# Graph attention layer on one core: another step order on TensorE, Gelu built from tanh, and LayerNorm 2's root on GpSimd

## The chip, the core and the metric

The kernel runs on one core of one Trainium2 chip. The metric is device time in microseconds (us). Five engines work side by side, each in the order of its own program, and wait for each other with semaphores: TensorE (PE, matmuls), VectorE (DVE), ScalarE (ACT), GpSimd (POOL) and SyncE (SP, here for DMAs). Matmuls write to PSUM, which ScalarE and VectorE read.

## What is computed

```
x = x + softmax(where(adj != 0, q k^T * SCALE, -inf)) v @ w_proj + b_proj     # 8 heads of 16, q k v = layer_norm(x, g1, be1) @ w_qkv
h2 = layer_norm(x, g2, be2)
out = x + gelu(h2 @ w1 + b1) @ w2 + b2                                        # gelu(approximate=True), the tanh form
# x is 4096 x 128 float32, adj 4096 x 4096 int32, w1 128 x 512
```

## The kernel before

A prologue normalises x, makes k and v for all 4096 rows and the first q (about 121 us). Then tiles `i` of 512 query rows follow (TILES = 8), and one more round without attention finishes the last tile. A tile has 64 steps `g` (STEPS): four pairs of heads times 16 steps, and each step handles two blocks of 128 keys (BLOCKS = 2).

In a step TensorE makes for each block the scores of a pair of heads, keys on partitions, by adding a mask (L1010, "masks", four matmuls that run together) and q times k (L1023, "scores"). ScalarE takes the exponential of each block (L639, 128x1024). Every second step in pairs 0, 1 and 3, and every fourth in pair 2, block 1 has no mask matmuls; GpSimd clamps and masks its exponentials instead (L496, L502, in `mask_probs`, and L490 in pair 0). The value matmuls (L918, "values", `weigh_values`) run three steps behind the scores (LAG = 3) and add up in `pv_ps`. Exponentials lie in eight slots of `probs`.

The exponentials subtract a row maximum found ahead of time: each step also has four "row units" (L853, `row`), q times k with query rows on partitions, over which VectorE takes a masked maximum (L677). They belong to a pair of heads 21 steps on (AHEAD), so those of the last steps belong to the next tile. GpSimd splits the maxima into two parts (`split_max`), and TensorE and ScalarE put them in the q stack ("shift").

Two rings of PSUM banks set the order. The score ring has two places (a pair of banks each), taken in turn by block 0, block 1 and, in some steps, a fill; the masks of a place wait until ScalarE has taken the place two before (`score_turn`). The row ring has three banks; a unit waits until VectorE has taken the one three places before. "Fills" are the rest of the work, placed by tables of step numbers. On the score ring (ACT_FILLS): shifts, the transposes of LayerNorm 2's output (h2t), the hidden units of the MLP (up, four of 128x512) and the next tile's q (q, four). On the row ring (DVE_FILLS): sums and their way back (normalisation of a pair), the projection (proj) and the second MLP layer (down, two). For tile i-1, attention's end, projection, LayerNorm 2 and MLP run in the first half of tile i: projection in step 7, LayerNorm 2's statistics on VectorE right behind it (`layer_norm_stats`), its root on ScalarE in step 9 (L650), its application on VectorE in step 10, up in steps 13, 15, 17 and 19, Gelu over all four in step 21 (L645), down in steps 23 and 25.

In its step TensorE's program reads: masks of both blocks, scores of both blocks, row units 0 and 1, values, ACT fill, row units 2 and 3, DVE fill.

ScalarE needs a table loaded for some functions: the exponential, the root and Gelu each bring an ACT_TABLE_LOAD when the one before was another.

## Time and profile before

| what | value |
|---|---|
| median of 3 runs | 1943.15 us (1942.3 to 1944.14) |
| profiled execution | 1946.16 us |
| its span, first to last instruction | 1944.4 us |
| mean granted TensorE clock | 0.959 of full speed |
| first exponential of attention | 121 us |

Busy time is the union of the instructions of an engine. A row of a group gives the count, the busy time, the mean length of one in ns, and behind the second bar the idle time of the engine before it with what ended it. In a timeline a row gives start, length, engine, line and operation, and merged repeats as x2, x8. A pair of exponentials reads as one row of 2.12 us.

### The profile page before, as it was taken

Reading aid. Unit: us, or ns where it says so; the run is one execution under the profiler, and the core shown is the slowest. Engines: PE = TensorE matmul, PEld = TensorE weight load, DVE = VectorE, ACT = ScalarE, POOL = GpSimd, SP = SyncE. Lnnn points to the kernel's source line nnn. Section 1 sums busy time; section 2 is a strip of 40 time slices with the busy share of each in tenths; the row PEclk is TensorE's granted clock in tenths of the full one; section 3 lists DMA queues with packets and bytes.
Section 4 is the critical chain, followed back from the end, with each engine's and each line's share of the span. In section 5 each row is a group of like instructions: output and inputs, shape, how many; then the busy total and the mean of one; then the engine's idle time right before and its main releaser. Section 6 shows DMA issues by size and latency. Waiting matters only on the chain.

```text
span 1944.4 us, 48355 instructions
## 1 busy us (share of the span) xinstructions
PE 1701.3 (87%) x18018; PEld 542.2 (28%) x18018; DVE 1456.3 (75%) x4495; ACT 1321.2 (68%) x1431; POOL 1128.1 (58%) x1058
## 2 busy tenths in 40 slices
PE   6988898889998889888998889888898889888876
PEld 3422222232232322322222322323223322223224
DVE  6888888768887588867887688876887678876601
ACT  4547777667767677676776677676776677766671
POOL 5945676437754476546764477545765477543340
PEclk9869999999999899999999999999999999999996
DMA  7700135002530034101440034200450024400000
GB/s 209 168 16 2 46 120 110 2 7 87 116 72 2 17 105 111 48 1 61 123 97 2 7 94 116 66 2 28 125 114 15 1 73 116 70 1 7 2 7 6
DMA packets 168705, 115.20 MB, mean 59 GB/s; under 512 B 139283, under 2 KB 149014, under 8 KB 168470
## 3 DMA queue, kind: packets, MB, share of 16 engines
q1 hardware_dynamic: 157718, 103.71, 21.8%
q10 hardware_dynamic: 10752, 8.39, 1.4%
q8 instruction: 143, 2.34, 0.5%
q14 instruction: 92, 0.75, 0.1%
HBM read 74.33 MB, written 4.19 MB: 40 GB/s over the span
## 4 chain that ended last, share of the span: by engine, by line
PE 44%; ACT 26%; issue 21%; DVE 8%; DMA 1%; ACTq 1%; SPq 0%; POOLq 0%; POOL 0%; DVEq 0%
ACT probs L639 21%; PE score_ps L1023 11%; PE score_ps L1010 8%; PE pv_ps L918 6%; PE ring_ps L853 5%; DVE masked_out L677 5%; PE ring_ps L974 2%; PE score_ps L941 2%; PE ring_ps L957 2%; PE ring_ps L951 2%; PE ring_ps L964 2%; PE score_ps L931 2%; ACT q_stack L535 1%; ACT hidden L604 1%; PE score_ps L877 1%
## 5 line engine op out<-in xcount | busy, mean ns | idle before, releaser
L677 DVE CUSTOM_DVE_ANT_0 masked_out<-ring_ps,row_mask 128x512 bf16<-128x512 f32 x2048 | 1328.2, 689 | 307.8 <-PE ring_ps L853 250.8
L639 ACT ACTIVATE probs<-score_ps,score_scale 128x1024 f32<-128x1024 f32 x1024 | 1084.6, 1110 | 501.6 <-PE score_ps L1023 488.3
L918 PE MATMUL pv_ps<-probs,v_ones 128*17 128x512 f32 x4096 | 552.0, 612 | 2.9 <-POOL probs L502 2.9
L496 POOL TENSOR_SCALAR probs<-probs 128x1024 f32<-128x1024 f32 x224 | 232.9, 1040 | 481.6 <-ACT probs L639 478.3
L502 POOL TENSOR_TENSOR probs<-probs,keep 128x1024 f32<-128x1024 f32 x224 | 478.2, 2135 | 40.7 <-POOL probs L496 28.9
L853 PE MATMUL ring_ps<-k_stack,q_stack 51*64 51x512 f16 x4096 | 455.6, 400 | 33.5 <-DVE row_max L677 33.1
L1010 PE MATMUL score_ps<-mask_t,ident_bf 64*64 64x512 bf16 x3200 | 331.9, 393 | 98.1 <-ACT probs L639 77.4
L1023 PE MATMUL score_ps<-q_stack,k_stack 51*64 51x512 f16 x4096 | 346.3, 396 | 66.1 <-ACT probs L639 37.8
L853 PEld LDWEIGHTS ring_ps<-k_stack,q_stack 51*64 51x64 f16 x4096 | 149.0, 106 | 481.9 <-DVE row_max L677 400.0
L1023 PEld LDWEIGHTS score_ps<-q_stack,k_stack 51*64 51x64 f16 x4096 | 103.6, 105 | 265.5 <-ACT probs L639 98.9
L677 DVE DVE_READ_ACCUMULATOR2_ANT row_max<- 128x1 f32 x2048 | 170.3, 83 | 0.0
L1010 PEld LDWEIGHTS score_ps<-mask_t,ident_bf 64*64 64x64 bf16 x3200 | 91.2, 105 | 246.6 <-ACT probs L639 191.1
L437 POOL TENSOR_SCALAR row_mask<-row_mask 128x1024 bf16<-128x1024 bf16 x124 | 129.6, 1045 | 23.9 <-POOL row_mask L433 23.9
L433 POOL TENSOR_SCALAR row_mask<-adj_in 128x1024 bf16<-128x1024 uint32 x124 | 128.9, 1040 | 12.3 <-DVE row_max L677 5.3
L918 PEld LDWEIGHTS pv_ps<-probs,v_ones 128*17 128x17 f32 x4096 | 68.4, 96 | 192.7 <-issue 186.1
L518 POOL TENSOR_TENSOR q_stack<-q_x,q_neg 128x512 f16<-128x512 f32 x28 | 32.5, 1160 | 63.1 <-ACT q_x L597 63.1
L442 POOL TENSOR_SCALAR max_unit<-neg_max 128x4 f32<-128x4 f32 x64 | 12.7, 198 | 95.0 <-DVE neg_max L687 90.1
L774 DVE RECIPROCAL recip<-ring_ps 128x8 f32<-128x8 f32 x32 | 6.5, 203 | 64.0 <-PE ring_ps L951 64.0
L535 ACT COPY q_stack<-score_ps 2x256 f16<-2x256 f16 x128 | 46.5, 363 | 9.5 <-PE score_ps L820 7.2
L974 PE MATMUL ring_ps<-w_sb,hidden 128*128 128x128 f32 x256 | 46.1, 335 | 2.8 <-DVE row_max L677 1.5
L788 DVE TENSOR_TENSOR rows<-ring_ps,x_res 128x256 f32<-128x256 f32 x16 | 6.8, 425 | 55.0 <-PE ring_ps L976 55.0
L490 POOL TENSOR_SCALAR keep<-mask_t 128x512 bf16<-128x512 bf16 x64 | 39.5, 617 | 5.5 <-ACT probs L639 0.2
(92 smaller groups left out, 894.5 us busy)
## 6 DMA issues: line engine op xcount, KB each, us to landing
adj_in<-adj SPq DMA_DIRECT2D x128, 512.0 KB, 4.1
xnT_dram<-attn ACTq DMA_DIRECT2D x8, 256.0 KB, 3.6
mask_t<-row_mask SPq DMA_TRANSPOSE x128, 3.4
xq<-xnT_dram ACTq DMA_DIRECT2D x8, 256.0 KB, 2.7
x_res<-x ACTq DMA_DIRECT2D x8, 256.0 KB, 3.6
out<-rows ACTq DMA_DIRECT2D x8, 256.0 KB, 2.3
w_sb<-L_gnn_w SPq DMA_DIRECT2D x2, 256.0 KB
probs<-x SPq DMA_DIRECT2D x1, 256.0 KB, 2.9
```

The lines of the kernel that those rows point to most:

```text
L433: nc.gpsimd.tensor_scalar(target, adj_in[:, half, :].bitcast(U32), 1.0, 0.0, ALU.min, ALU.max)\
L437: nc.gpsimd.tensor_scalar(target, target, BIG, -BIG, ALU.mult, ALU.add).then_inc(mask_done, 1)
L496: nc.gpsimd.tensor_scalar(flat, flat, 128.0, 0.0, ALU.min, ALU.max).then_inc(probs_bounded, 1)
L502: nc.gpsimd.tensor_tensor(view, view, keep[:, m // 4, :].unsqueeze(1).broadcast_to([128, 2, TILE]), ALU.mult).then_inc(probs_masked, 1)
L535: last = nc.scalar.copy(stack[r:r + SHIFT_PARTS, p, 256 * jj:256 * (jj + 1)], bank.bitcast(F16)[r:r + SHIFT_PARTS, 0:256])
L639: nc.scalar.activation(probs[:, (2 * g + n) % SLOTS, :], score_ps[:, half:half + 2, :].rearrange("p a n -> p (a n)"), ACT.Exp, scale=score ...
L677: nc.vector.tensor_tensor_reduce(out=masked_out[:, place % 3, :], in0=ring_ps[:, place % 3, :], in1=row_mask[:, j, ch * 512:(ch + 1) * 512 ...
L853: last = nc.tensor.matmul(ring_ps[64 * t:64 * (t + 1), place % 3, :], stack[rows, p, first:first + 64], k_stack[rows, p, ch, K_FIRST:], st ...
L918: last = nc.tensor.matmul(pv_ps[32 * k:32 * k + HD + 1, :], v_ones[:, BLOCKS * (g % QUARTER) + b, 2 * p + a, :], probs[:, (2 * g + b) % SL ...
L974: nc.tensor.matmul(bank[:, 128 * s:128 * (s + 1)], hidden[:, f, 128 * t:128 * (t + 1)], w2_sb[:, f, :], start=(f == 0), stop=False)
L1010: last = nc.tensor.matmul(bank[to, :], ident_bf[keys, keys], mask_t[keys, source, :], start=True, stop=False)
L1023: last = nc.tensor.matmul(bank[64 * t:64 * (t + 1), :], k_stack[rows, p, m // 4, at + 64 * t:at + 64 * (t + 1)], q_stack[par][rows, p, :], ...
```

## The change

- In a step TensorE issues block 0's masks, row units 0 and 1, block 0's scores, block 1's masks and scores, row units 2 and 3, then values and both fills.
- Gelu is no longer one function of ScalarE over 128x2048. Per hidden unit f, ScalarE writes z = h + b (`hidden`) and z squared (`bent`), GpSimd makes z (0.7979 + 0.0357 z^2) (`bend`, two operations of 128x512), ScalarE takes tanh of it two steps later, GpSimd makes z (0.5 tanh + 0.5) (`gate`, two operations). In the last round, without attention, ScalarE's Gelu stays.
- LayerNorm 2's 1/sqrt: VectorE makes a first guess from the bits of var + eps (two operations), GpSimd runs three Newton steps of four operations on 128x4 (`root2`). VectorE applies it two subtiles in step 10, two in step 11.
- Fills move: up to steps 15, 17, 19, 21; h2t to 12 and 13; down to 27 and 29; q to 28, 31, 34 and 40. The load of x for the residual moves from step 0 to 2, the aggregates of LayerNorm 2 to the head of step 8, the store to 30.

TensorE, an even and an odd step of a middle tile without fills. L1010 or L1091 are masks, L1023 or L1104 scores, L853 or L934 row units, L918 or L999 values, each row with four matmuls per block or pair of units. Before:

```order
L1010 MATMUL score_ps<-mask_t,ident_bf 64x512 x8
L1023 MATMUL score_ps<-q_stack,k_stack 64x512 x8
L853 MATMUL ring_ps<-k_stack,q_stack 64x512 x4
L918 MATMUL pv_ps<-probs,v_ones 17x512 x4
L853 MATMUL ring_ps<-k_stack,q_stack 64x512 x4
L1010 MATMUL score_ps<-mask_t,ident_bf 64x512 x4
L1023 MATMUL score_ps<-q_stack,k_stack 64x512 x8
L853 MATMUL ring_ps<-k_stack,q_stack 64x512 x4
L918 MATMUL pv_ps<-probs,v_ones 17x512 x4
```

And of the change:

```order
L1091 MATMUL score_ps<-mask_t,ident_bf 64x512 x4
L934 MATMUL ring_ps<-k_stack,q_stack 64x512 x4
L1104 MATMUL score_ps<-q_stack,k_stack 64x512 x4
L1091 MATMUL score_ps<-mask_t,ident_bf 64x512 x4
L1104 MATMUL score_ps<-q_stack,k_stack 64x512 x4
L934 MATMUL ring_ps<-k_stack,q_stack 64x512 x4
L999 MATMUL pv_ps<-probs,v_ones 17x512 x4
L1091 MATMUL score_ps<-mask_t,ident_bf 64x512 x4
L934 MATMUL ring_ps<-k_stack,q_stack 64x512 x4
L1104 MATMUL score_ps<-q_stack,k_stack 64x512 x8
L934 MATMUL ring_ps<-k_stack,q_stack 64x512 x4
L999 MATMUL pv_ps<-probs,v_ones 17x512 x4
```

The values no longer stand between the two pairs of row units, and block 1's masks stand behind block 0's scores.

GpSimd of the change, steps 18 to 20 of a middle tile (before, only the probs and max rows are there). `bent` and `hidden` rows at L523 and L526 are a bend, at L534 and L537 a gate; the probs rows are one masked block, the max rows a split:

```order
L523 TENSOR_SCALAR bent<-bent 128x512
L526 TENSOR_TENSOR bent<-bent,hidden 128x512
L534 TENSOR_SCALAR bent<-bent 128x512
L537 TENSOR_TENSOR hidden<-bent,hidden 128x512
L508 TENSOR_SCALAR probs<-probs 128x1024
L514 TENSOR_TENSOR probs<-probs,keep 128x1024
L454 TENSOR_SCALAR max_unit<-neg_max 128x4
L458 CAST max_part<-max_unit 128x4
L461 TENSOR_TENSOR max_part<-max_unit,max_part 128x4
L523 TENSOR_SCALAR bent<-bent 128x512
```

A bend and a gate now stand in front of the masked block of their step. ScalarE of the change around the same place, where before one Gelu stood between two table loads:

```order
L707 ACTIVATE probs<-score_ps,score_scale 128x1024 x2
L668 ACTIVATE hidden<-score_ps,b_col 128x512
L669 ACTIVATE bent<-score_ps,b_col 128x512
L715 ACTIVATE bent<-bent 128x512
L707 ACTIVATE probs<-score_ps,score_scale 128x1024 x2
```

No table load stands in the order of the change between the first exponential and the last round.

The step tables:

```diff
-ACT_FILLS = {11: ("h2t", 0), 12: ("h2t", 1), 24: ("q", 0), 27: ("q", 1), 33: ("q", 2), 40: ("q", 3)}
-ACT_FILLS.update({13 + 2 * f: ("up", f) for f in range(FC)})
+UP_STEPS = [15 + 2 * f for f in range(FC)]
+ACT_FILLS = {12: ("h2t", 0), 13: ("h2t", 1), 28: ("q", 0), 31: ("q", 1), 34: ("q", 2), 40: ("q", 3)}
```

GpSimd, the root and the calls in its step loop:

```diff
+            def root2(i):
+                first = (i - 1) * ROOT_OPS
+                pool.wait_ge(ln2_step, (i - 1) * LN2_STEPS + LN2_STATS)
...
+                for k in range(NEWTON):
...
+                    nc.gpsimd.tensor_tensor(newton[:, :], rstd[:, :], rstd[:, :], ALU.mult).then_inc(root_step, 1)
+                    pool.wait_ge(root_step, first + 4 * k + 1)
...
+                    if d and g == AGGR_STEP:
+                        root2(i)
+                    if d and c and g - 1 in UP_STEPS:
+                        bend(i, bcd, UP_STEPS.index(g - 1))
+                    if d and c and g - 3 in UP_STEPS:
+                        gate(i, UP_STEPS.index(g - 3))
```

ScalarE:

```diff
+                elif what[0] == "up" and bcd[1]:
+                    f = what[1]
+                    n = (i - 1) * FC + f
+                    if n >= 2:
+                        act.wait_ge(gelu_done, n - 1)
+                    nc.scalar.activation(hidden[:, f, :], bank, ACT.Identity, bias=b1_col[:, f:f + 1])
+                    nc.scalar.activation(bent[:, f % 2, :], bank, ACT.Square, bias=b1_col[:, f:f + 1])\
+                      .then_inc(score_taken, 1)
...
-                    if d and c and g == GELU_STEP:
-                        nc.scalar.activation(hidden[:, :, :].rearrange("p f n -> p (f n)"),
-                                             hidden[:, :, :].rearrange("p f n -> p (f n)"),
-                                             ACT.Gelu_apprx_tanh).then_inc(gelu_done, 1)
-                    if d and g == SQRT_STEP:
-                        act.wait_ge(ln2_step, (i - 1) * LN_STEPS + LN_STATS)
-                        nc.scalar.activation(rstd[:, :], inv_var[:, :], ACT.Sqrt).then_inc(rstd_done, 1)
+                    if d and c and g - 2 in UP_STEPS:
+                        f = UP_STEPS.index(g - 2)
+                        act.wait_ge(bent_done, 2 * ((i - 1) * FC + f) + 2)
+                        nc.scalar.activation(bent[:, f % 2, :], bent[:, f % 2, :], ACT.Tanh).then_inc(tanh_done, 1)
```

TensorE's step:

```diff
                 for g in range(STEPS):
                     if c:
-                        for n in range(BLOCKS):
-                            masks(g, n)
-                        for n in range(BLOCKS):
-                            scores(g, n)
+                        masks(g, 0)
                     for x in range(UNITS // 2):
+                        row(g, x)
+                    if c:
+                        scores(g, 0)
+                        masks(g, 1)
+                        scores(g, 1)
+                    for x in range(UNITS // 2, UNITS):
                         row(g, x)
...
                         weigh_values(i, bcd, g - LAG)
                     if g in act_fills:
                         act_fill(i, bcd, g, act_fills[g])
-                    for x in range(UNITS // 2, UNITS):
-                        row(g, x)
                     if g in dve_fills:
                         dve_fill(i, bcd, g, dve_fills[g])
```

## Rows read from the trace of the kernel before

**Rows 1.** The page, busy time of the engines.

```profile
PE 1701.3 (87%) x18018; PEld 542.2 (28%) x18018; DVE 1456.3 (75%) x4495; ACT 1321.2 (68%) x1431; POOL 1128.1 (58%) x1058
```

**Rows 2.** The page's groups, ScalarE's exponentials: busy, mean ns, idle before.

```profile
L639 ACT ACTIVATE probs<-score_ps,score_scale 128x1024 f32<-128x1024 f32 x1024 | 1084.6, 1110 | 501.6 <-PE score_ps L1023 488.3
```

**Rows 3.** Timeline, two plain steps: start, length, instruction, idle before.

```profile
954.45 0.39 PE L853 MATMUL ring_ps<-k_stack,q_stack 51*64 51x512 f16 x4
954.47 2.12 ACT L639 ACTIVATE probs<-score_ps,score_scale 128x1024 f32<-128x1024 f32 x2 [0.80 <-PE score_ps L1023]
...
954.77 1.05 PE L918 MATMUL pv_ps<-probs,v_ones 128*17 128x512 f32 x8
955.02 0.69 DVE L677 CUSTOM_DVE_ANT_0 masked_out<-ring_ps,row_mask 128x512 bf16<-128x512 f32 x1 [0.29 <-issue]
...
955.75 0.43 PE L853 MATMUL ring_ps<-k_stack,q_stack 51*64 51x512 f16 x4
...
955.99 0.40 PE L1010 MATMUL score_ps<-mask_t,ident_bf 64*64 64x512 bf16 x4
...
956.64 0.63 PE L1023 MATMUL score_ps<-q_stack,k_stack 51*64 51x512 f16 x8 [0.25 <-ACT probs L639]
...
957.16 2.12 ACT L639 ACTIVATE probs<-score_ps,score_scale 128x1024 f32<-128x1024 f32 x2 [0.58 <-PE score_ps L1023]
...
960.08 2.12 ACT L639 ACTIVATE probs<-score_ps,score_scale 128x1024 f32<-128x1024 f32 x2 [0.80 <-PE score_ps L1023]
```

**Rows 4.** Line L645, Gelu: lengths, first and last start.

```profile
L645 ACT ACTIVATE hidden<-hidden x7: 1910/1912/1914, 407.0 to 1758.3; 128x2048 f32<-128x2048 f32 x7
```

**Rows 5.** Timeline of TensorE, the fills.

```profile
792.56 1.05 PE L951 MATMUL ring_ps<-sum_sel,attn 128*128 128x2 f32 x8
...
803.11 3.84 PE L964 MATMUL ring_ps<-wp_pad,attn 128*128 128x128 f32 x32 [0.21 <-DVE row_max L677]
...
836.23 1.12 PE L941 MATMUL score_ps<-h2T,w_sb 128*128 128x512 f32 x2
...
868.52 1.16 PE L974 MATMUL ring_ps<-w_sb,hidden 128*128 128x128 f32 x8
...
870.02 1.16 PE L974 MATMUL ring_ps<-w_sb,hidden 128*128 128x128 f32 x8
```

**Rows 6.** Timeline, LayerNorm 2's statistics on VectorE.

```profile
806.99 0.69 DVE L781 TENSOR_TENSOR x_res<-ring_ps,x_res 128x512 f32<-128x512 f32 x1 [2.62 <-PE ring_ps L964]
...
809.51 0.69 DVE L677 CUSTOM_DVE_ANT_0 masked_out<-ring_ps,row_mask 128x512 bf16<-128x512 f32 x1
```

**Rows 7.** Timeline, GpSimd's masking, the root's table load, units; behind Gelu.

```profile
815.10 2.12 POOL L502 TENSOR_TENSOR probs<-probs,keep 128x1024 f32<-128x1024 f32 x1 [0.17 <-issue]
815.23 1.28 ACT L639 ACT_TABLE_LOAD   x1
...
818.73 0.40 PE L853 MATMUL ring_ps<-k_stack,q_stack 51*64 51x512 f16 x2 [2.56 <-DVE row_max L677]
...
866.12 1.91 PE L918 MATMUL pv_ps<-probs,v_ones 128*17 128x512 f32 x8
```

**Rows 8.** Line L331, LayerNorm's application: ns min/median/max.

```profile
L331 DVE TENSOR_SCALAR rows<-x_res,mean_var,rstd x32: 333/335/2059, 362.5 to 1915.2; 128x128 f32<-128x128 f32 x32
```

**Rows 9.** The page's groups, GpSimd.

```profile
L496 POOL TENSOR_SCALAR probs<-probs 128x1024 f32<-128x1024 f32 x224 | 232.9, 1040 | 481.6 <-ACT probs L639 478.3
L502 POOL TENSOR_TENSOR probs<-probs,keep 128x1024 f32<-128x1024 f32 x224 | 478.2, 2135 | 40.7 <-POOL probs L496 28.9
...
L518 POOL TENSOR_TENSOR q_stack<-q_x,q_neg 128x512 f16<-128x512 f32 x28 | 32.5, 1160 | 63.1 <-ACT q_x L597 63.1
```

**Rows 10.** Timeline, a small operation of GpSimd.

```profile
821.39 0.19 POOL L446 CAST max_part<-max_unit 128x4 f16<-128x4 f32 x1 [0.17 <-POOL max_unit L442]
```

**Rows 11.** Busy us (x count) by window, with granted clock (PEclk).

```profile
954.00:960.00 6.00, 5.47 (x72) 1.36 (x68) 5.64 (x19) 4.23 (x4) 3.62 (x4) 1.00 0.62 200
862.00:870.00 8.00, 5.52 (x38) 1.98 (x38) 3.63 (x11) 4.94 (x5) 2.07 (x2) 0.79 0.00 0
```

More of the change, by code:

```diff
@@ L602, in take_fill @@
                                          scale=gb[:, 2:3], bias=gb[:, 3:4]).then_inc(score_taken, 1)
+                elif what[0] == "up" and bcd[1]:
+                    f = what[1]
+                    n = (i - 1) * FC + f
+                    if n >= 2:
[3 more added lines that the diff above has]
+                      .then_inc(score_taken, 1)
                 elif what[0] == "up":
-                    nc.scalar.activation(hidden[:, what[1], :], bank, ACT.Identity if bcd[1] else ACT.Gelu_apprx_tanh,
+                    nc.scalar.activation(hidden[:, what[1], :], bank, ACT.Gelu_apprx_tanh,
                                          bias=b1_col[:, what[1]:what[1] + 1]).then_inc(score_taken, 1)
@@ L784, in take_fill @@
                     dve.wait_ge(row_taken, full)
-                    layer_norm_stats(lambda k: dve.wait_ge(ln2_step, (i - 1) * LN_STEPS + k), ln2_step, x_res)
+                    for s in range(SUB):
+                        nc.vector.bn_stats(stats[:, s, :], x_res[:, s, :]).then_inc(ln2_step, 1)
                 elif what[0] == "down":
@@ L795, in body @@
                 for g in range(STEPS):
[L796 to L798 removed]
+                    if d and g == AGGR_STEP:
+                        before = (i - 1) * LN2_STEPS
+                        dve.wait_ge(ln2_step, before + SUB)
+                        for s in range(SUB):
+                            nc.vector.bn_aggr(mean_var[:, s, :], stats[:, s, :]).then_inc(ln2_step, 1)
+                        dve.wait_ge(ln2_step, before + 2 * SUB)
+                        nc.vector.tensor_scalar(inv_var[:, :], mean_var[:, :, 1], EPS, None, ALU.add).then_inc(ln2_step, 1)
+                        dve.wait_ge(ln2_step, before + 2 * SUB + 1)
+                        nc.vector.tensor_scalar(half_bits[:, :], inv_var[:, :].bitcast(I32), 1, None,
+                                                ALU.logical_shift_right).then_inc(ln2_step, 1)
+                        dve.wait_ge(ln2_step, before + 2 * SUB + 2)
+                        nc.vector.tensor_scalar(rstd[:, :].bitcast(I32), half_bits[:, :], -1.0, ROOT_GUESS,
+                                                ALU.mult, ALU.add).then_inc(ln2_step, 1)
+                    if d and g in (APPLY_STEP, APPLY_STEP + 1):
+                        dve.wait_ge(root_step, i * ROOT_OPS)
+                        for s in range(2 * (g - APPLY_STEP), 2 * (g - APPLY_STEP + 1)):
+                            nc.vector.tensor_scalar(rows2[:, s, :], x_res[:, s, :], mean_var[:, s, 0:1], rstd[:, s:s + 1],
+                                                    ALU.subtract, ALU.mult).then_inc(ln2_step, 1)
                     if g < row_steps(b, c):
```

64 lines of the change are left out of this document (51 added, 13 removed).

## The prediction

> **What bounds the kernel now.** I read the page first. No engine is full: TensorE 87% busy by the modelled ends of its matmuls, VectorE 75%, ScalarE 68% [rows 1]. ScalarE's dearest group, the 1024 exponentials, waited 501.6 us, nearly all of it for the score matmuls [rows 2]. So an in-order handshake sets the time, and the timeline of a stretch without extra work has to be read.
>
> There [rows 3] a step is two exponentials (the pair 2.12 us), four row units and eight value matmuls. Exponential pairs start at 954.47, 957.16 and 960.08: steps of 2.69 and 2.92, mean 2.80. The cycle: both exponentials end, then the scores start on TensorE (956.64, released by ACT), then 0.52 us to the next exponential (957.16). TensorE issues both blocks' masks ahead of both scores, so block 0's scores wait for block 1's exponential of the step before: ScalarE idles 0.58 or 0.80 us in each step.
>
> Gelu's rows lie 225.2 us apart (407.0 to 1758.3, six intervals) [rows 4]: a middle tile. Its 64 steps at 2.80 make 179.2; the other 46.0 us are the work between steps (LayerNorm, MLP, next q, normalisation) and the waits it causes: VectorE's normalisation [rows 6], and ScalarE's tables and Gelu [rows 4, 7].
>
> **The new order, plain steps.** Now TensorE does: masks 0, row units 0 and 1, scores 0, masks 1, scores 1, units 2 and 3, values. The old wait is gone: scores 0 need only exponential 0 of the step before. What is late next? Unit 3 needs the bank of unit 0 (ring of three), and the values stand behind it. From the same rows: units start to first maximum 0.57 (954.45 to 955.02); the maximum 0.69; its end to the next units about 0.06 (955.71 to 955.75, the second half a little later); units to values 0.32 (954.45 to 954.77); values to next work 0.98 (to 955.75); masks to units 0.24 (taken from units to masks, 955.75 to 955.99). Sum 2.86 us for either kind of step. Before, the values lay between the two pairs of units and hid this round trip; now only scores and masks do (0.72 to 0.96 us of the 1.32). ScalarE fits: exponential 0 starts 0.76 after the units, exponential 1 ends at 2.88, the masks that need it come at 2.86 + 0.48. VectorE has 0.3 us left per step. So the reorder by itself gains nothing: 64 x 2.86 = 183.0, which is 3.8 worse.
>
> **Between the steps.** TensorE's work is unchanged, but now lies wholly on its path. From starts and durations [rows 5], less 0.07 for the overlap of modelled ends, as the values' 1.05 stand for 0.98 [rows 3]: a 512-column float32 fill 1.05 (1.12 less 0.07), eight of these (hidden, q) 8.4; sums 0.98 and their way back, taken the same and 0.07 on top, 8.2 for four (0.98 + 1.05 each); projection 3.8; second MLP layer 1.5 for each half of a fill (868.52 to 870.02), two fills, 6.0; transposes of h 0.7 and of shifts 1.7 (estimates: both are smaller than a fill, and a shift's next mask waits 0.2 for exponential 1). Together 28.8.
>
> Waits per tile:
> - LayerNorm 2's statistics on VectorE. From the addition to the first maximum 2.52 us (806.99 to 809.51) [rows 6]. Three small operations now follow the aggregates instead of two: + 0.2. Measured from the projection's end the maximum starts 2.8 later instead of 0.8: + 2.0.
> - The root. Removed: table, root, table on ScalarE. Added: 12 dependent 128x4 operations on GpSimd. A small one there takes 0.19 behind a wait of 0.17 for its forerunner [rows 10], 0.36, so 4.4 us with a hand-over. VectorE needs it two steps on, 5.4 us after the guess: covered. But GpSimd's masking of step 7 is queued behind it, 1.04 + 2.14 [rows 9], its half-size mask operation (about 0.6) and gaps = 4.2 more, and the values of step 7 wait for it in step 10: done 8.7 to 9.0 after the guess, wanted at 6.8. Take + 2.2 (bounds 0 and 4).
> - Normalising now in two halves, 0.6 each instead of one block, but see the lock below: inside that 2.2.
> - Hidden units: Identity and Square on ScalarE (0.6 to 0.7 each, estimated from Gelu's 1.91 for four times the columns plus a start-up) hold the score bank 1.4 instead of 0.8 us; the next masks 1 wait, and units 3 come 0.35 late, three times: + 1.0. The q fills hold it 1.3: + 0.5.
> - GpSimd's bend and gate. A 128x512 tensor_scalar lies between half of the 1024 form's 1.04 and all of it, and I take 0.6; for the tensor_tensor I take 1.16, the nearest row, between 1.07 (half of the 1024 form) and its whole 2.14 [rows 9]. With gaps a bend or gate is 2.1, so a pair of steps holds 4.2 + 3.4 for its masking = 7.6 us, against 7.1 (two steps and one fill and its wait). Four such rounds and a split (1.1) eat most of the 3.8 us of slack that a masked block has: + 1.5 (bounds 0 and 8).
> - TensorE's clock: it waited 2.56 us before 818.73, and behind Gelu the granted clock of the stretch was 0.79 [rows 11], eight value matmuls taking 1.91 instead of 1.05 (866.12) [rows 7]; that is the 1.2 GHz level for part of the stretch. The Gelu wait goes; the 2.5 us wait after the projection stays or grows. + 1.5 (bounds 0 and 3).
> Sum 8.7. Gone altogether are Gelu's 1.91 [rows 4] and four table loads of 1.28 (815.23 is one) [rows 7], 7.0 of ScalarE in a tile, and TensorE's stalls behind them.
>
> A tile: 183.0 + 28.8 + 8.7 = 220.5 against 225.2, so -4.7; six of them -28. The first tile has neither LayerNorm 2 nor MLP: it gains around its fills what it does not lose by 0.06 a step, -3 (estimate). In the last attention tile 20 steps have no row units; there nothing holds the values back, and ScalarE's 2.12 plus a short hand-over gives 2.2 instead of 2.80: -12, with -4 for the rest. The tail, on its own path, trades one root operation for 4.4 us: +4. Sum -43. The profiled execution took 1946.16 us (span 1944.4), 3 over the median; 1943.15 - 43 = 1900.
>
> **Two rules weighed.** A normalising tensor_scalar on VectorE has a median of 0.335 us and a maximum of 2.06 [rows 8]; GpSimd's tensor_tensor ran from 815.10 to 817.22 and TensorE waited until 818.73 for the row maxima queued behind the normalisation [rows 7]. The Trainium skill (SBUF — State Buffer, Who interferes with whom) says that such a VectorE operation and a GpSimd one exclude each other for the whole instruction; this trace agrees with 2.06 against 0.335. More GpSimd work means more such meetings: the two halves could each meet one.
> A table load takes 1.28 us in the row at 815.23 [rows 7]. The Trainium skill (ScalarE: Activation LUTs, What ACT_TABLE_LOAD costs) counts 2.66 for a switch with its drain. By that the tile would gain 5.5 us more (four times 1.38); I go by the row.
>
> **Rivals.**
> - GpSimd becomes the bound (slower). Place: steps 16 to 26, where a weigh waits for masked exponentials queued behind bends and gates, with ScalarE waiting for gates too. For it: 7.6 against 7.1 already; against: 58% busy over all, and the first two rounds start idle. If a float32 tensor_tensor costs 2.14, a round is 9.6 and four rounds lag 10, of which slack takes the first two: +8 a tile over my sum, seven tiles, 1956. It decides once bend and gate average above 2.9 us each.
> - The lock catches both halves: the first waits up to 2.1, beyond the 2.2 already counted 1.7, the second as much: 3.4 x 7 = 24, 1924.
> - TensorE's clock falls in ordinary steps, since it now pauses 0.4 to 0.6 us in each. A slow step costs about 1.5 more (values 1.91); every eighth step slow is 12 a tile: 1985. Against: the present plain stretch pauses as long per step, at clock 1.00 [rows 11].
> - The round trip is not on the path, since units 2 are issued early and the modelled ends hide overlap; then VectorE bounds, four maxima at 0.69 less 0.03 to 0.07 of overlap each, about 2.65: 0.2 x 450 steps, 1810. Against it: the ring of three banks leaves unit 3 no other bank, and the second pair starts 0.04 after the first maximum's end [rows 3].
>
> **Chances.** Forecast 0.66 (its bounds alone: 1878 to 1925), lock on both halves 0.12, faster still 0.06: together faster 0.84. GpSimd as the bound 0.08 and the clock 0.04: slower 0.12. Same 0.04, for a part of the GpSimd case that just eats the gain; a measurement of this kernel tells 0.2% (3.9 us) from no change. The range takes in the lock case and the near side of the GpSimd and faster cases: 1866 to 1938.
>
> **What would show it.** Plain steps of 2.86 us without alternation, exponentials starting before the earlier pair is done, "TensorE's row units wait for row_max" as the largest wait of TensorE; no Gelu or root tables in the middle; a wait of values for GpSimd's probs in steps 10 and 24. Plain steps of 2.65 or above 3.0 would make the forecast wrong, as would values waiting for GpSimd more than 5 us a tile.

## The result, and the profile after

The changed kernel takes 1914.43 us (median of 4 runs, 1913.38 to 1916.23), the kernel before 1943.64 on the same chips (4 runs, 1942.3 to 1946.99): a ratio of 0.9846, 95% interval 0.9834 to 0.9859. Forecast were 1900 us and a range of 1866 to 1938. The time is in the range, 14 us above the forecast. The profiled execution of the changed kernel took 1913.38 us, its span 1911.6, 32.8 shorter than the span before.

The page of the changed kernel, busy time of the engines and the largest groups with their waits (it answers to [rows 1], [rows 2] and [rows 9]):

```profile
PE 1737.2 (91%) x18018; PEld 547.8 (29%) x18018; DVE 1431.6 (75%) x4503; ACT 1298.9 (68%) x1443; POOL 1252.4 (66%) x1266
...
L707 ACT ACTIVATE probs<-score_ps,score_scale 128x1024 f32<-128x1024 f32 x1024 | 1087.8, 1112 | 457.3 <-PE score_ps L1104 454.8
...
L999 PE MATMUL pv_ps<-probs,v_ones 128*17 128x512 f32 x4096 | 542.6, 602 | 11.4 <-POOL probs L514 11.4
...
L934 PEld LDWEIGHTS ring_ps<-k_stack,q_stack 51*64 51x64 f16 x4096 | 168.3, 106 | 287.7 <-DVE row_max L742 242.1
...
L1104 PEld LDWEIGHTS score_ps<-q_stack,k_stack 51*64 51x64 f16 x4096 | 102.7, 104 | 341.6 <-PE score_ps L1091 325.3
```

Only 44 us of the exponentials' wait are gone (501.6 to 457.3). TensorE's busy share rose from 87 to 91% in a shorter span. GpSimd is 124 us busier and still not the bound.

The changed kernel's timeline, one plain step from exponential to exponential (it answers to [rows 3]; start, length, instruction, and in brackets the idle time before it with its releaser):

```profile
939.33 0.38 PE L934 MATMUL ring_ps<-k_stack,q_stack 51*64 51x512 f16 x2
...
939.39 2.12 ACT L707 ACTIVATE probs<-score_ps,score_scale 128x1024 f32<-128x1024 f32 x2 [0.76 <-PE score_ps L1104]
...
939.95 0.40 PE L934 MATMUL ring_ps<-k_stack,q_stack 51*64 51x512 f16 x2 [0.24 <-DVE row_max L742]
...
940.28 1.05 PE L999 MATMUL pv_ps<-probs,v_ones 128*17 128x512 f32 x8
...
941.27 0.41 PE L1091 MATMUL score_ps<-mask_t,ident_bf 64*64 64x512 bf16 x4
...
941.51 0.39 PE L934 MATMUL ring_ps<-k_stack,q_stack 51*64 51x512 f16 x4
...
941.75 0.11 PEld L1104 LDWEIGHTS score_ps<-q_stack,k_stack 51*64 51x64 f16 x4 [0.34 <-PE score_ps L1091]
...
942.07 0.69 DVE L742 CUSTOM_DVE_ANT_0 masked_out<-ring_ps,row_mask 128x512 bf16<-128x512 f32 x1 [0.34 <-issue]
942.27 1.11 ACT L707 ACTIVATE probs<-score_ps,score_scale 128x1024 f32<-128x1024 f32 x1 [0.76 <-PE score_ps L1104]
```

The step is 2.88 us (939.39 to 942.27), in even and odd steps alike (2.88 or 2.89). Unit 3 waits for the maximum (0.24), then 0.33 to the values, 0.99 to the next masks, 0.24 to the units: the path that the prediction summed. The row it had no term for is the weight load of the scores, which waits for the masks' end: masks start at 941.27, their scores at 941.75.

The changed kernel's timeline, TensorE's waits in steps 8 to 10 of the same tile as [rows 7]:

```profile
794.76 0.40 PE L934 MATMUL ring_ps<-k_stack,q_stack 51*64 51x512 f16 x2 [1.67 <-DVE row_max L742]
...
801.33 0.40 PE L934 MATMUL ring_ps<-k_stack,q_stack 51*64 51x512 f16 x2 [0.55 <-DVE row_max L742]
...
802.95 1.05 PE L999 MATMUL pv_ps<-probs,v_ones 128*17 128x512 f32 x8 [1.22 <-POOL probs L514]
```

Where the 32.8 us went, by the first exponential of each tile in the two traces, and from the start of the last pair to the end (us):

```
                        before   after   difference
up to tile 0             121.2   117.6      -3.6   (the same code; 117.2 to 123.4 in the runs below)
tile 0                   205.2   202.6      -2.6
tiles 1 to 6            1351.6  1330.4     -21.2   (-3.5 a tile)
tile 7                   215.1   205.5      -9.6
last exponentials to end  51.3    55.5      +4.2
```

Within an average middle tile: steps 0 to 7 +0.4, steps 8 to 11 -0.3, steps 12 to 19 +1.7 (bends and gates), steps 20 to 34 -3.7 (no Gelu load), steps 35 to 63 -1.6.

The last view is the windows. Before, the first row is steps 8 to 11 of tile 3, the second steps 20 to 26, the third tiles 1 to 6 (columns: us, busy time and count of PE, PEld, DVE, ACT and POOL, granted clock, DMA share, GB/s):

```profile
807.90:824.40 16.50, 12.57 (x130) 3.31 (x122) 14.54 (x46) 11.80 (x13) 5.84 (x8) 0.90 0.01 1
852.10:885.30 33.20, 28.68 (x302) 11.85 (x294) 19.81 (x61) 21.20 (x22) 12.41 (x8) 0.95 0.03 9
326.00:1678.00 1352.00, 1202.77 (x13327) 372.46 (x13321) 1065.21 (x3271) 953.70 (x1008) 817.17 (x746) 0.98 0.25 61
```

The same stretches of the changed kernel:

```profile
792.30:808.90 16.60, 12.76 (x124) 2.88 (x120) 14.65 (x49) 8.46 (x8) 11.45 (x23) 0.90 0.00 1
838.20:861.80 23.60, 22.23 (x264) 6.86 (x260) 18.15 (x58) 17.90 (x22) 21.49 (x20) 1.00 0.01 2
320.00:1651.00 1331.00, 1232.22 (x13332) 378.63 (x13326) 1044.91 (x3277) 935.97 (x1021) 921.90 (x913) 0.99 0.25 62
```

The second stretch is not as much shorter as it looks: fills that stood in it now stand behind it, and steps 20 to 34 together give 3.7 us.

The trace's record of the clock is finer than two digits and knows two levels. TensorE ran at 1.2 GHz instead of 2.4 for stretches that sum to a lost clock (half their length) of 32.4 us in tiles 1 to 6 before and 10.2 after; in the whole span 80.5 and 48.5, the rest mostly in the prologue and the tail. Before, such a stretch lies behind the wait of 2.56 us in step 10 [rows 7] and behind that of Gelu; after, one follows the waits of steps 8 to 11 in five of tiles 1 to 6. The difference, 3.7 us a tile, is as large as the gain of a tile. Whether it was its cause, the experiments had to say.

### The profile page after: what moved, and what is told of

The parts are those of the page before. It is cut to its first block and busy times, and to the rows that moved or that the text cites. A ratio compares the mean times of both kernels' runs of the same rounds, so it can differ in the third digit from the quotient of the medians.

```text
span 1911.6 us, 48585 instructions
## 1 busy us (share of the span) xinstructions
PE 1737.2 (91%) x18018; PEld 547.8 (29%) x18018; DVE 1431.6 (75%) x4503; ACT 1298.9 (68%) x1443; POOL 1252.4 (66%) x1266
## 3 DMA queue, kind: packets, MB, share of 16 engines
q1 hardware_dynamic: 157718, 103.71, 22.2%
## 5 line engine op out<-in xcount | busy, mean ns | idle before, releaser
L742 DVE CUSTOM_DVE_ANT_0 masked_out<-ring_ps,row_mask 128x512 bf16<-128x512 f32 x2048 | 1298.9, 687 | 248.2 <-PE ring_ps L934 207.0
L707 ACT ACTIVATE probs<-score_ps,score_scale 128x1024 f32<-128x1024 f32 x1024 | 1087.8, 1112 | 457.3 <-PE score_ps L1104 454.8
L934 PE MATMUL ring_ps<-k_stack,q_stack 51*64 51x512 f16 x4096 | 533.4, 390 | 76.3 <-DVE row_max L742 75.5
L999 PE MATMUL pv_ps<-probs,v_ones 128*17 128x512 f32 x4096 | 542.6, 602 | 11.4 <-POOL probs L514 11.4
L1104 PE MATMUL score_ps<-q_stack,k_stack 51*64 51x512 f16 x4096 | 387.7, 401 | 28.5 <-ACT q_x L657 6.0
L1091 PE MATMUL score_ps<-mask_t,ident_bf 64*64 64x512 bf16 x3200 | 333.9, 397 | 25.2 <-ACT bent L669 11.2
L934 PEld LDWEIGHTS ring_ps<-k_stack,q_stack 51*64 51x64 f16 x4096 | 168.3, 106 | 287.7 <-DVE row_max L742 242.1
L1091 PEld LDWEIGHTS score_ps<-mask_t,ident_bf 64*64 64x64 bf16 x3200 | 94.4, 104 | 384.2 <-ACT probs L707 310.6
L1104 PEld LDWEIGHTS score_ps<-q_stack,k_stack 51*64 51x64 f16 x4096 | 102.7, 104 | 341.6 <-PE score_ps L1091 325.3
L999 PEld LDWEIGHTS pv_ps<-probs,v_ones 128*17 128x17 f32 x4096 | 68.2, 95 | 141.2 <-issue 122.2
L548 POOL TENSOR_TENSOR newton<-rstd 128x4 f32<-128x4 f32 x24 | 4.8, 200 | 85.4 <-DVE rstd L873 82.6
L523 POOL TENSOR_SCALAR bent<-bent 128x512 f32<-128x512 f32 x28 | 17.4, 620 | 46.5 <-ACT bent L669 45.3
L842 DVE TENSOR_TENSOR attn<-ring_ps,attn 128x512 f32<-128x512 f32 x32 | 22.1, 692 | 29.7 <-PE ring_ps L1038 29.7
```

The costliest lines, as they stand in the source:

```text
L707: nc.scalar.activation(probs[:, (2 * g + n) % SLOTS, :], score_ps[:, half:half + 2, :].rearrange("p a n -> p (a n)"), ACT.Exp, scale=score ...
L742: nc.vector.tensor_tensor_reduce(out=masked_out[:, place % 3, :], in0=ring_ps[:, place % 3, :], in1=row_mask[:, j, ch * 512:(ch + 1) * 512 ...
L934: last = nc.tensor.matmul(ring_ps[64 * t:64 * (t + 1), place % 3, :], stack[rows, p, first:first + 64], k_stack[rows, p, ch, K_FIRST:], st ...
L999: last = nc.tensor.matmul(pv_ps[32 * k:32 * k + HD + 1, :], v_ones[:, BLOCKS * (g % QUARTER) + b, 2 * p + a, :], probs[:, (2 * g + b) % SL ...
L1091: last = nc.tensor.matmul(bank[to, :], ident_bf[keys, keys], mask_t[keys, source, :], start=True, stop=False)
L1104: last = nc.tensor.matmul(bank[64 * t:64 * (t + 1), :], k_stack[rows, p, m // 4, at + 64 * t:at + 64 * (t + 1)], q_stack[par][rows, p, :], ...
```

## The experiments

Times are medians; ratios are to the kernel before, run on the same chip.

### The new order alone

```diff
# the kernel before, TensorE's loop only
-                        for n in range(BLOCKS): masks(g, n)
-                        for n in range(BLOCKS): scores(g, n)
+                        masks(g, 0)
                     row units 0 and 1
+                    scores(g, 0); masks(g, 1); scores(g, 1)
+                    row units 2 and 3
                     values, fills
-                    row units 2 and 3
```

> The kernel before with TensorE's new step order alone: Gelu from its table and LayerNorm 2's root on ScalarE, as before. Theory (from the two traces): a plain step goes from 2.69/2.91 alternating (mean 2.80) to 2.89 every time, since each step now holds the whole round trip units, maximum, units once; that is +0.085 us for some 330 plain steps, +28 us, against some -10 in the last tile (its steps without row units get shorter) and what the even step saves at the fills. So no gain: 1940 to 1955 us. Rival: the new order carries the measured gain (it lets the exponentials start before the pair of maxima is done) and the other two parts only remove table loads that cost little: 1915 to 1925 us.

Measured: 1951.66 us, 1.0032 (1.002 to 1.0043). The order by itself is slower, as the prediction said ("the reorder by itself gains nothing"); the rival falls. A middle tile takes 226.7 us instead of 225.3 (means of tiles 1 to 6), and its lost clock is 6.2 us instead of 5.4.

### Everything but the order

```diff
# the kernel after, TensorE's loop as before: the diff above, reversed
```

> The kernel after with TensorE's old step order (the Gelu from tanh and the root on GpSimd stay). Theory: the gain of the change comes from these two parts, which take the table loads and the long waits out of the steps 8 to 25; plain steps alternate 2.69/2.91 again, the last tile is 10 us longer: 1900 to 1925 us. Rival (the order carries the gain): within 10 us of the kernel before, 1933 to 1950 us.

Measured: 1939.35 us, 0.9967 (0.9955 to 0.998). My theory falls here: without the new order the two other parts win 4 us, not 25. Together the two halves of the change win 33 us more than the sum of each alone (1951.7 + 1939.4 - 1943.6 = 1947.5, against 1914.4). The wait that the order hides is seen in this kernel's timeline, step 10:

```profile
810.90 1.91 PE L999 MATMUL pv_ps<-probs,v_ones 128*17 128x512 f32 x8 [3.47 <-POOL probs L514]
```

The values wait 3.47 us for GpSimd's masking instead of 1.22, and take 1.91 instead of 1.05: half clock.

### A shorter maximum

```diff
# the kernel after, row_maximum
-                    out=masked_out[:, place % 3, :], in0=ring_ps[:, place % 3, :],
-                    in1=row_mask[:, j, ch * 512:(ch + 1) * 512], ...
+                    out=masked_out[:, place % 3, 0:256], in0=ring_ps[:, place % 3, 0:256],
+                    in1=row_mask[:, j, ch * 512:ch * 512 + 256], ...
```

> The kernel after with each row maximum taken over the first 256 of its 512 columns (it leaves out half of the columns of every maximum; VectorE's instruction gets shorter, the order and every wait stay). Theory: the round trip units to maximum to units is what closes a plain step, and it runs through one maximum of 0.69 us; with it at about 0.42 the step shrinks from 2.89 to 2.6 to 2.73 and the whole kernel to 1805 to 1830 us. Rival: a plain step is as long as TensorE's or ScalarE's own work in it (the trip is hidden beside the exponentials): less than 20 us gained, over 1895 us.

Measured: 1836.24 us, 0.9444 (0.9421 to 0.9467). A maximum takes 423 ns, plain steps 2.73 and 2.61 us in turn. The rival of less than 20 us falls: the maximum is on the path. By itself that would also fit a kernel bound by VectorE's own work; against this stands that VectorE idles 0.34 us in each plain step of the changed kernel, until the next units are there (942.07 above), so it is the whole round trip. The total missed the expected 1805 to 1830 by 6, since the steps around the fills shrink less (steps 20 to 34 of a middle tile by 1.1 us, fifteen plain ones would by some 3). The page of this kernel:

```profile
L742 DVE CUSTOM_DVE_ANT_0 masked_out<-ring_ps,row_mask 128x256 bf16<-128x256 f32 x2048 | 784.4, 423 | 637.4 <-PE ring_ps L934 538.6
...
L934 PEld LDWEIGHTS ring_ps<-k_stack,q_stack 51*64 51x64 f16 x4096 | 159.6, 107 | 170.7 <-DVE row_max L742 121.9
```

### The values in two halves

```diff
# the kernel after, TensorE's step
 masks 0, row units 0 and 1, scores 0
+values of block 0 (two matmuls of four)
 masks 1
-scores 1, row units 2 and 3, values of both blocks
+row units 2 and 3, scores 1, values of block 1 (the other two)
```

> The kernel after, where TensorE's step is split evenly: masks of block 0, row units 0 and 1, scores 0, the half of the values that block 0 of three steps ago fed, then masks of block 1, row units 2 and 3, scores 1, the other half of the values. Same work, every wait for a row maximum has a half of the values ahead of it. Theory: the round trip (0.57 from the units' end to the maximum, two maxima of 0.69, 0.06 back) stays covered by TensorE's own work, and a step becomes as long as VectorE's four maxima or TensorE's instructions, about 2.70: -0.19 us for some 400 steps, about 1825 to 1850 us; the wait of PE's weight loads for row_max shrinks from 242 us to under 100. Rival: the wait for masks (0.48 us from the masks' end to the scores that add to them) or for the exponentials takes its place, and the step stays within 0.05 of 2.89: 1895 to 1930 us.

Measured: 2188.65 us, 1.1249 (1.1231 to 1.1267): it is over 250 us above both expectations. The row units' weight loads do wait less for row_max, as hoped (34.7 us instead of 242.1), but TensorE is 96% busy. Its page and its timeline of one step:

```profile
PE 2109.6 (96%) x18018; PEld 579.4 (26%) x18018; DVE 1460.2 (67%) x4503; ACT 1350.0 (62%) x1443; POOL 1250.1 (57%) x1266
...
L934 PEld LDWEIGHTS ring_ps<-k_stack,q_stack 51*64 51x64 f16 x4096 | 126.7, 106 | 245.2 <-issue 184.4
```

```profile
1065.39 1.04 PE L1001 MATMUL pv_ps<-probs,v_ones 128*17 128x512 f32 x4
1066.36 0.41 PE L934 MATMUL ring_ps<-k_stack,q_stack 51*64 51x512 f16 x4
1066.60 0.39 PE L1107 MATMUL score_ps<-q_stack,k_stack 51*64 51x512 f16 x4
1066.92 1.04 PE L1001 MATMUL pv_ps<-probs,v_ones 128*17 128x512 f32 x4
```

A half of the values (four records, two matmuls) takes 0.97 us to the next work (1065.39 to 1066.36), and the whole (eight records) takes 0.99 in the changed kernel (940.28 to 941.27). The four value matmuls, 17 columns each, write to four different strips of partitions; two of them cost as much as four, so the four run side by side. The split doubled the price: 0.97 us more TensorE time in each of 512 steps, of which 274 us came out as time (2188.65 against 1914.43). The Trainium skill (TensorE: Matmul & The Clock Gate, Part 3: Packing small matmuls — row/col tiling, The mechanism) says that matmuls at different tile positions of the array overlap; this pair of rows agrees.

### Zeros in the waits of the kernel before

The clock was now the suspect, so it was tried by itself: nothing made quicker, only the idle array kept busy.

```diff
# the kernel before, TensorE
+def add_zeros(count):    # four matmuls of 17 columns side by side, adding 0 to pv_ps
+    for k in range(4 * count):
+        to = 32 * (k % 4)
+        nc.tensor.matmul(pv_ps[to:to + HD + 1, :], ident_bf[:, 0:HD + 1], zero_bf[:, :], start=False, stop=False)
 for g in range(STEPS):      # the zeros in tiles 1 to 7 only
+    if g == 23: add_zeros(9)
     ...
     for x in range(UNITS // 2, UNITS):
+        if g == 10 and x == 3: add_zeros(11)
         row(g, x)
```

> The kernel before with matmuls added that add zeros to the accumulator of the values, placed in TensorE's two long idle stretches of every middle tile: eleven groups of four (about 2.3 us) in step 10 ahead of the last row unit, where it waits 2.56 us, and nine (1.9 us) ahead of step 23's masks, where it waits 2.25 us. No wait is shortened and nothing useful is done. Theory (from the clock records of the four kernels so far: TensorE ran at half clock for long enough to lose 81.5 us in the kernel before, 93.6 with the new order alone, 72.8 with the two other parts alone, 49.5 in the kernel after; against the sum of the single parts both together win 33 us more, and the clock loses 35 less): the clock that falls behind each of these waits costs 1.7 us each time, so filling them gives back up to 5.4 us in each of the tiles 1 to 6: 1905 to 1922 us, with no half clock in steps 10, 11, 22 and 23. Rival: the half clock lies beside waits that would be there anyway, or the zeros delay as much as they give: 1936 to 1955 us.

Measured: 1919.23 us, 0.987 (0.9853 to 0.9887). 24.2 us come from multiplying zeros; no half clock is left in tiles 1 to 6. The timeline of the kernel before behind Gelu, then of this one:

```profile
863.89 0.41 PE L1010 MATMUL score_ps<-mask_t,ident_bf 64*64 64x512 bf16 x4 [2.25 <-ACT probs L639]
864.89 0.87 PE L1023 MATMUL score_ps<-q_stack,k_stack 51*64 51x512 f16 x8 [0.59 <-ACT probs L639]
```

```profile
850.57 2.12 PE L1033 MATMUL pv_ps<-zero_bf,ident_bf 128*17 128x512 bf16 x36
852.89 0.41 PE L1012 MATMUL score_ps<-mask_t,ident_bf 64*64 64x512 bf16 x4 [0.20 <-ACT probs L641]
853.89 0.63 PE L1025 MATMUL score_ps<-q_stack,k_stack 51*64 51x512 f16 x8 [0.59 <-ACT probs L641]
854.35 0.39 PE L855 MATMUL ring_ps<-k_stack,q_stack 51*64 51x512 f16 x4
854.66 1.05 PE L920 MATMUL pv_ps<-probs,v_ones 128*17 128x512 f32 x8
```

The masks start as late as before (11.8 us after step 20's first exponential in both), so the zeros shortened no wait. What is shorter is the work behind: scores 0.63 instead of 0.87, values 1.05 instead of 1.91. The Trainium skill (TensorE: Matmul & The Clock Gate, What's actually happening) puts the penalty of the clock's ramp, for modelling, at under 1% of a typical kernel's span. One ramp fits that here (1.7 or 3.4 us of lost clock), but in this kernel the clock has to come up two times in each of seven tiles, and the time that filling the waits gave back, 24.2 of 1943.4 us or 1.2%, is above it.

### The root alone back on ScalarE

```diff
# the kernel after
-  VectorE: half_bits, first guess; GpSimd: root2(i), three Newton steps
+  VectorE: nc.vector.reciprocal(inv_var); ScalarE, step 9: nc.scalar.activation(rstd, inv_var, ACT.Sqrt)
```

> The kernel after with LayerNorm 2's root back on ScalarE (two table loads and the root between the exponentials of step 9 and step 10); the new order and Gelu from tanh stay. Theory: steps 8 to 11 are those of the kernel with the order alone, 20.9 us against 16.1, with two idle stretches of 1.6 and 3.4 us and half clock behind both: +4.8 us in seven tiles, 1940 to 1952 us; the root on GpSimd is what the new order needs. Rival: ScalarE's table loads are hidden beside GpSimd's chain to the values (8.6 us from the root's start, which now is gone), and only the lock of the shared port counts: 1908 to 1920 us.

Measured: 1924.79 us, 0.9901 (0.9885 to 0.9918), 10 above the changed kernel and between the two expectations. Steps 8 to 11 cost 1.5 us a tile more, not 4.8, and the lost clock is 0.9 us a tile higher; the tail is 4.1 shorter (51.4 us). My figure had come from the kernel with the order alone, which also normalises all rows at once, right beside GpSimd's masking; that this is what made it too high is not tested.

### Gelu alone back on ScalarE

```diff
# the kernel after (Gelu in step 23 here, in step 21 in the kernel before; the expectation names 21)
-  ScalarE: Identity, Square, Tanh; GpSimd: bend, gate
+  ScalarE: Identity; step 23: nc.scalar.activation(hidden, hidden, ACT.Gelu_apprx_tanh)
```

> The kernel after with Gelu back on ScalarE's table, in step 21; the new order and the root on GpSimd stay. Theory: steps 12 to 19 get 1.2 us shorter (no tanh, bending or gates), steps 20 to 34 2.6 longer (the loads and the wait of 2.1 us behind them, with half clock): +1.4 a tile, 1918 to 1930 us. Rival: the gain of the change comes mainly from the Gelu's table loads, 1935 to 1948 us.

Measured: 1934.31 us, 0.9956 (0.994 to 0.9972), 20 above the changed kernel: just under the rival, above the theory. Steps 12 to 19 are 2.0 us shorter and steps 20 to 34 4.7 longer; one wait of 2.97 us stands in step 24 with 2.9 us of lost clock a tile behind it, in place of none.

### Two groups of values moved

```diff
# the kernel after: values of step 8 ahead of row units 2 and 3; those of step 10 into step 11
+                        if g == APPLY_STEP + 1: weigh_values(i, bcd, APPLY_STEP - LAG)   # behind scores(g, 0)
+                    if g == AGGR_STEP and c: weigh_values(i, bcd, g - LAG)               # ahead of units 2 and 3
```

> The kernel after with two groups of values moved in TensorE's order: step 8's stand ahead of the row units 2 and 3 (which wait 1.67 us for maxima queued behind LayerNorm 2's statistics), and step 10's, which wait 1.22 us for GpSimd's masking, stand in step 11 behind block 0's scores. Theory: 0.98 us of work goes into the first wait, 0.72 and more into the second, and the half clock behind them (1.7 us in most tiles) goes too: -1.7 to -4 us in eight tiles, 1885 to 1902 us. Rival: the exponentials of step 11 wait for the later values as long as was won, the chain through GpSimd sets steps 8 to 11 as before: 1908 to 1920 us.

Measured: 1913.11 us, 0.9836 (0.9821 to 0.9851), the rival's figure: not to be told from the changed kernel. The long waits did go (in steps 8 to 11 of the tile shown none is over 0.7 us, in the others none over 0.9), and those steps take 15.9 us instead of 16.6; tiles 1 to 6 are 4.4 us shorter in the trace, which the spread of the prologue (117.2 to 123.4) hides in the total. But the clock fell all the same, in five of these six tiles. The timeline of this kernel in step 8, and a window right behind:

```profile
800.44 0.40 PE L934 MATMUL ring_ps<-k_stack,q_stack 51*64 51x512 f16 x2 [0.57 <-DVE row_max L742]
800.45 0.61 PE L1091 MATMUL score_ps<-mask_t,ident_bf 64*64 64x512 bf16 x4
801.05 0.40 PE L934 MATMUL ring_ps<-k_stack,q_stack 51*64 51x512 f16 x2
801.66 0.40 PE L934 MATMUL ring_ps<-k_stack,q_stack 51*64 51x512 f16 x2 [0.21 <-DVE row_max L742]
```

```profile
803.70:808.70 5.00, 4.73 (x42) 0.98 (x36) 4.76 (x13) 2.89 (x3) 4.33 (x6) 0.76 0.00 2
```

The clock fell at 802.69. TensorE looks busy ahead of that, but its program is held up by the row units: one of two matmuls whenever VectorE frees a bank, every 0.61 us, with masks and scores between them. A long idle row is not the only thing that stood ahead of a fall; a thinly filled stretch did too.

### Zeros in the three other kernels

```diff
# add_zeros as above, a group is four matmuls
# the kernel after:     7 groups ahead of unit 3 of step 8, 2 of step 10; 5 ahead of step 10's values
# the order alone:      7 groups ahead of unit 3 of step 8, 15 of step 10; 9 ahead of step 23
# all but the order:    3 groups ahead of unit 3 of step 8; 16 ahead of step 10's values
```

> The kernel after with groups of four matmuls that add zeros to the values' accumulator, in its waits of the middle tiles and the last one: seven ahead of step 8's last row unit (wait 1.67 us), two ahead of step 10's (0.55), five ahead of step 10's values (1.22). Nothing useful is done. Theory (half clock behind idle stretches is worth its full time): the kernel after still loses 10 us to half clock in its tiles 1 to 6 (steps 8, 10, 11) and some 2 in the last: 1900 to 1909 us. Rival (what is left of the half clock comes from thinly filled stretches, which the zeros don't reach): 1911 to 1918 us.

> The kernel before with the new step order alone and the same kind of zeros in its three long waits: seven groups ahead of step 8's last row unit (1.58 us), fifteen ahead of step 10's (3.39), nine ahead of step 23's masks (2.09). Theory: the order alone came out at 1951.7 us only because its waits are lumped and the clock falls behind each; 37.5 us of half clock in tiles 1 to 6 and some 4 in the last come back: 1906 to 1918 us, so at full clock the order alone is worth -1 to -13 us against the kernel before with zeros (1919.2). Rival: the order itself costs 0.085 us in a plain step and 3.4 us a tile in steps 8 to 11, clock or no clock: 1925 us or more.

> The kernel after with TensorE's old step order and zeros in its wait for GpSimd's masking (sixteen groups ahead of step 10's values, 3.47 us; three ahead of step 8's last row unit, 0.84 us). Theory: 17.1 us of half clock in tiles 1 to 6 and some 3 in the last come back: 1917 to 1925 us. With the three other kernels with zeros the two parts then add up (after with zeros = order with zeros + rest with zeros - before with zeros, within 5 us), where without zeros they missed by 33 us. Rival: the parts still help each other by 15 us and more at full clock, through GpSimd's chain.

Measured, with the lost clock of tiles 1 to 6 in brackets (none is left where zeros were added):

```
                       without zeros        with zeros    zeros give
before                 1943.6 (32.4)          1919.2         24.4
order alone            1951.7 (37.5)          1920.0         31.7
all but the order      1939.4 (17.1)          1934.0          5.4
both (the change)      1914.4 (10.2)          1911.4          3.0
both, less the sum of the single parts:  -33.1         -23.4
```

(The kernel before came out between 1943.4 and 1944.5 beside these runs.)

The ratios are 0.9824 (0.9808 to 0.9839), 0.9864 (0.9845 to 0.9884) and 0.9937 (0.992 to 0.9954). The order alone with zeros came 2 us above its expected range and below the 1925 of its rival. The other two went by their rivals: the zeros are worth only 3.0 us in the changed kernel (interval overlapping that without them), and 5.4 where 17.1 us of clock was lost.

The zeros also fill the waits of tile 7, which lost 5.1, 8.5, 5.1 and 0.0 us of clock without them. Tile by tile in the traces, which leaves out the prologue and its spread, tiles 1 to 7 are 26.3, 33.6, 5.5 and 5.8 us shorter with zeros, for 37.5, 46.1, 22.2 and 10.2 us of lost clock. So lost clock is not time lost: in the kernel before, and with the order alone, it cost some 0.7 of its size, with everything but the order a quarter. Why it is cheaper there is open; that TensorE's work was not what ended those steps would explain it, but no run tested that. In the changed kernel 3.5 of the 5.8 us are tile 5, where the profiled execution without zeros had two extra waits of 1.7 us.

And the parts still help each other by 23 us at full clock (in the traces 2.7 of them stand in the prologue, where the code is the same, and are chance).

The place of most of that help is steps 8 to 11. With zeros, and so at full clock, they take 15.6 us before, 17.5 with the order alone, 17.0 with the rest alone and 15.6 with both: 3.3 less than the parts' sum, 20 us in six tiles. The timelines of ScalarE show one side of it, the kernel with the order alone first, then the kernel before:

```profile
816.86 1.28 ACT L650 ACT_TABLE_LOAD   x1
```

```profile
813.71 1.28 ACT L650 ACT_TABLE_LOAD   x1
```

Counted from step 8's first exponential (809.02 and 807.89) the root's load starts at 7.84 instead of 5.82: the root on ScalarE stands behind step 9's exponentials, which the new order makes 2 us later here. On GpSimd the root starts 1.9 us after that exponential in either order, and TensorE's 1.67 us of waiting in step 8 run beside it; with the old order the same chain is met in one wait of 3.47. This is read from the traces; no run took this part away by itself.

### The last tile's root back on ScalarE

```diff
# the kernel after with zeros
-                    if d and g == AGGR_STEP: root2(i)
+                    if c and d and g == AGGR_STEP: root2(i)
+                    if d and not c and g == 9: nc.scalar.activation(rstd, inv_var, ACT.Sqrt)
```

> The kernel after with zeros in its waits (1911.4 us), and LayerNorm 2's root of the last tile alone back on ScalarE, where no exponentials follow it; in the other tiles it stays on GpSimd. Theory: the tail from the last pair of exponentials to the end is 55.5 to 56.9 us with the root on GpSimd (twelve small operations, 4.4 us in a row) and 51.3 to 53.1 with it on ScalarE, whose table load has cover there: 1905 to 1909 us. Rival: the tail is longer for another reason and stays over 55 us: 1910 to 1913 us.

Measured: 1907.05 us (5 runs, 1905.7 to 1909.49), 0.9811 (0.9788 to 0.9833): the fastest version, in the expected range; its interval ends just below that of the changed kernel (0.9834 to 0.9859). The last exponentials to the end take 52.4 us, with the root on GpSimd and the same zeros 56.7.

## Why the prediction was right, step by step

- **Plain step.** Predicted 2.86 us without alternation, measured 2.88 to 2.89. Two of its signs were wrong: exponentials don't start before the earlier pair is done (ScalarE idles 0.76 us ahead of every pair, as a pair of 2.12 in a step of 2.86 must), and the wait for row_max (242.1 us) is not TensorE's largest; that for the masks' end is (325.3), and the masks' own wait for the exponentials is larger too (310.6), though both mostly lie beside the round trip. That the round trip through the maximum closes the step is shown by the shorter maximum, together with VectorE's idle 0.34 us. "The reorder by itself gains nothing" is shown: the order alone is 0.3% slower.
- **Middle tile.** Predicted -4.7, measured -3.5. The sum of 220.5 compares with 221.7 (mean) in the trace. The values' wait for GpSimd came in step 10 as said, 1.22 us inside its term of 2.2, and not in step 24; the statistics' wait is the 1.67 in step 8. The two operations of a bend or gate take 0.62 and 1.27 instead of 0.6 and 1.16, with the gap 2.1 as predicted.
- **First tile, tail.** Predicted -3 and +4, measured -2.6 and +4.2; that the tail's +4 is the root is shown by the two kernels that moved it back.
- **Last tile.** Predicted -16, measured -9.6. The step of the prediction that failed: "ScalarE's 2.12 plus a short hand-over gives 2.2 instead of 2.80". The 20 steps without row units went from 58.4 to 52.5 us, fills included, 0.3 a step instead of 0.6. The 2.2 came only where GpSimd masks block 1 (2.17); steps with masks for both blocks take 2.51 to 2.81 even without a fill. Scores wait for the end of their own masks, which I had no term for; in a plain step the round trip hides it, here it is on the path, twice where both blocks have masks. The changed kernel's timeline there, a step of 2.17:

```profile
1818.45 0.41 PE L1091 MATMUL score_ps<-mask_t,ident_bf 64*64 64x512 bf16 x4
1818.93 0.30 PEld L1104 LDWEIGHTS score_ps<-q_stack,k_stack 51*64 51x64 f16 x8 [0.37 <-PE score_ps L1091]
1818.93 0.63 PE L1104 MATMUL score_ps<-q_stack,k_stack 51*64 51x512 f16 x8
```

  It is 0.48 us from masks to scores. Outside these 20 steps the tile gave 3.7, near the predicted 4, and as much as zeros alone gave there in the kernel before (3.6).
- **The clock.** Predicted +1.5 a tile in the changed kernel, measured 1.7 of lost clock, and 1.0 of time by the zeros in tiles 1 to 6. What I missed is the other side: the kernel before loses 5.4 a tile, and [rows 11] showed it (0.79). I left it inside "TensorE's stalls behind them", where its size did not show. The runs size it: of 29.2 us, zeros alone give 24.4 in the kernel before and 3.0 in the changed one, so some 21 us of the gain are clock and 8 are left at full clock (1919.2 to 1911.4). The rows put those 8 in the last tile (-5.8) and tiles 0 to 6 (about -8), against the longer tail (+5.4).
- **The cause of the gain.** That removed loads and the new order would work apart from each other was a tacit step, and it failed: apart they give +8 and -4. The sum held because it was made for both together. That it came so near in a middle tile is in part luck: 3.7 us of lost clock went, a quantity that the sum held in a word and not in a number.
- **Rivals.** GpSimd did not become the bound: the value matmuls waited 11.4 us for it in all, their weight loads 17.7. The lock (the meeting with GpSimd under "Two rules weighed") met both halves of the normalisation in the tile shown, but for 1.06 and 1.21 us; once, in tile 5, it took 2.19, and that tile lasted 224.3 us instead of 220.5 to 221.9; line L878's total is that of L331 before (21.6 and 20.9 us), so its 24 us did not come. The clock did not fall in plain steps. Steps of 2.65 did not come; a plain step with a shorter maximum comes near it.
- **The total.** The sum for the profiled execution was -43, measured -32.8: +6.4 from the last tile, +7 from six tiles at 1.2, +0.6 from the first tile and the tail, -3.6 from the prologue, whose code is unchanged and whose length varies between runs.

## What to carry to other kernels

Where TensorE waits a few microseconds once per stretch (1.6 to 3.5 here), read the granted clock behind the wait, not over the span: in this kernel that clock was worth more than the wait's removal, and useless matmuls in the wait bought most of it. Two parts of a change that meet in the same few steps can be worth nothing apart and 1.5% together, so undo each part both from the old and from the new kernel. Before splitting matmuls to hide a wait, check whether they run side by side in the array.

## What was not expected of the hardware

- TensorE's waits were followed by stretches at 1.2 GHz, mostly of 3.4 or 6.8 us: all fourteen waits of 2.25 and 2.56 us in tiles 1 to 7 of the kernel before, but only two of the seven waits of 1.67 us in step 8 of the changed kernel directly. Filled with zeros, none was. A stretch with one unit each 0.61 us stood ahead of a fall with no wait over 0.6 us.
- Four value matmuls of 17 columns take 0.99 us together and two of them 0.97.
- Scores that add to their masks' banks start 0.48 us after the masks start, though the masks' own issue takes 0.24.
